# Four cross attentions of a perceiver: new orders of the steps in the masked and plain ones, one query operand for all, values one group at a time

## The reference

```python
q = split_heads(query @ wq_kernel + wq_bias)         # query: layernorm of x
k = split_heads(key @ wk_kernel + wk_bias)           # key, value: context, 4096 tokens
v = split_heads(value @ wv_kernel + wv_bias)
scores = jnp.einsum('bhqd,bhkd->bhqk', q, k) / jnp.sqrt(jnp.float32(HD))
scores = jnp.where(m == 0, jnp.float32(-1000000000.0), scores)   # layer 1: m = mask
attn = jax.nn.softmax(scores, axis=-1)
out = jnp.einsum('bhqk,bhkd->bhqd', attn, v)
return out @ wo_kernel + wo_bias
```

## Time and profile before

| | us |
|---|---|
| median of three runs | 1549.96 |
| lowest, highest run | 1547.44, 1559.05 |
| the profiled execution, as timed | 1559.34 |
| its span in the trace | 1558.1 |
| PE busy | 1348.7 (87%) |
| DVE busy | 1008.2 (65%) |
| ACT busy | 849.9 (55%) |
| POOL busy | 518.1 (33%) |

### The profile page before, as it was taken

The page is one execution under the profiler, slowest core; times in us unless marked ns, Lnnn a source line. Parts: engine busy times, 40 slices in busy tenths (PEclk is TensorE's granted clock), DMA queues, the critical chain, the costliest instruction groups (busy, mean ns, idle before and its releaser), DMA issues. The chain is left out here.

```text
span 1558.1 us, 28950 instructions
## 1 busy us (share of the span) xinstructions
PE 1348.7 (87%) x10520; PEld 684.5 (44%) x10594; DVE 1008.2 (65%) x2341; ACT 849.9 (55%) x1302; POOL 518.1 (33%) x700
## 2 busy tenths in 40 slices
PE   6879999799999888599999888599998895999987
PEld 3536567233333356234444455234444582344445
DVE  3524656899999634678886043588885236888832
ACT  1121211799999621189999451167777211777762
POOL 1322011498998810655665330111110002111100
PEclk8989999699999887699999899779999996899999
DMA  6376787111114020111113146112225201112400
GB/s 212 117 223 213 218 252 240 55 43 42 46 36 130 1 68 1 45 52 47 50 49 121 62 120 212 49 37 58 61 62 187 68 0 37 52 52 56 119 2 7
DMA packets 115679, 136.35 MB, mean 88 GB/s; under 512 B 13729, under 2 KB 96841, under 8 KB 113490
## 3 DMA queue, kind: packets, MB, share of 16 engines
q1 hardware_dynamic: 100434, 117.95, 24.4%
q10 hardware_dynamic: 15104, 16.56, 3.7%
HBM read 99.55 MB, written 34.87 MB: 86 GB/s over the span
## 5 line engine op out<-in xcount | busy, mean ns | idle before, releaser
L1150 ACT ACTIVATE prob_a<-ps 128x1024 f32<-128x1024 f32 x464 | 457.5, 1021 | 131.3 <-PE ps L978 90.6
L960 PE MATMUL ps<-kop,qop 52*128 52x512 f16 x1024 | 312.1, 418 | 57.2 <-DVE best_a L1174 19.1
L1174 DVE TENSOR_REDUCE best_a<-ps 128x1 f32<-128x512 f32 (+1 forms) x488 | 315.2, 709 | 52.5 <-PE ps L960 52.2
L978 PE MATMUL ps<-qop,kop 52*128 52x256 f16 x2048 | 246.6, 281 | 6.3 <-ACT prob_a L1150 3.7
L1007 PE MATMUL ps<-prob_a,vop_a 128*32 128x256 f32 x3072 | 211.9, 414 | 7.7 <-ACT qop L1090 3.1
L960 PEld LDWEIGHTS ps<-kop,qop 52*128 52x128 f16 x1024 | 77.0, 95 | 266.8 <-DVE best_a L1174 92.7
L1170 DVE CUSTOM_DVE_ANT_0 dump_a<-ps,neg_q 128x512 bf16<-128x512 f32 (+1 forms) x244 | 163.6, 715 | 43.3 <-PE ps L960 42.0
L1288 POOL TENSOR_TENSOR used_a<-prob_a,gT 128x1024 f32<-128x1024 f32 x64 | 153.0, 2391 | 27.9 <-DVE used_a L1187 17.0
L1266 POOL TENSOR_SCALAR mrest_a<-nmax_a 128x2 f32<-128x2 f32 x64 | 27.8, 434 | 354.2 <-DVE nmax_a L1179 352.9
L978 PEld LDWEIGHTS ps<-qop,kop 52*128 52x128 f16 x2048 | 96.4, 96 | 95.2 <-issue 30.8
L554 ACT ACTIVATE kp<-ps,bk 128x512 f16<-128x512 f32 x64 | 43.8, 687 | 171.1 <-PE ps L486 156.7
(11 more groups left out here) (367 smaller groups left out, 1783.7 us busy)
## 6 DMA issues: line engine op xcount, KB each, us to landing
kop<-kparts SPq DMA_DIRECT2D x384, 64.0 KB, 2.3
vals<-vst SPq DMA_DIRECT2D x16, 1024.0 KB, 4.4
kparts<-kp SPq DMA_DIRECT2D x64, 256.0 KB, 2.3
vraw<-vals SPq DMA_DIRECT2D x64, 256.0 KB, 3.0
e_w<-in_e_w SPq DMA_DIRECT2D x4, 2048.0 KB, 11.8
z_w<-in_z_w SPq DMA_DIRECT2D x24, 256.0 KB, 6.8
ctxT<-in_ctxT SPq DMA_DIRECT2D x8, 512.0 KB, 12.3
raw<-in_mask ACTq DMA_DIRECT2D x16, 256.0 KB, 4.1
```

The costliest lines, as they stand in the source:

```text
L960: return pe.matmul(out, qop[rows, h, t * P:(t + 1) * P], kop[rows, h % UNROLL, first:first + CHUNK], start=True, stop=True)
L978: ins = pe.matmul(st_bank(n)[:, j * NT:(j + 1) * NT], kop[rows, h % UNROLL, at:at + P], qop[rows, h, :], start=(j % 2 == 0), stop=(not add ...
L1150: act.activation(prob[:, n % NP, :], st_bank(n), ACT.Exp, scale=1.0 / SCORE_UNIT).then_inc(S("exp_done"), 1)
L1174: dve.tensor_reduce(out, bank, AX.X, ALU.max).then_inc(sem, 1)
```

## The change

1. The order strings of the masked and the plain attention are new, and with them `SUM_AT` and `TURN_AT` (after which exponential ACT reads the sums and places the maxima). In the plain one values come one group at a time in four places ("v") and two by two ("vv") in two.
2. The masked attention shields two groups a head, not three: g = 1 and 5. The third gets two mask matmuls instead (L983).
3. `qop` is one tile for all layers, set to zero once, by POOL, in `project_context`. For layers 1 to 3 only the rows that hold more than loads write are cleared, by two small DMAs of zeros from DRAM (`clear_rows`), and PE waits for them before its first product, and in layer 2 for the row of ones of the mask too, for which SP waited at its end before.
4. Queries that see no key get zeros in the query operand. In layer 0 POOL multiplies the whole of `qop` (4096 values a partition) by a 0/1 tile at the end of `project_context`. In layer 1 DVE first writes the masked sum to `whole` (two instructions), ACT copies it into the high part and DVE subtracts for the low part.
5. The mask's number is -2^27, not -2^100, in the cross attentions.

```diff
-MASKED_ORDER = "CCK CCK CCK CVV CCK KCCKF CKCT KCCC VV".replace(" ", "")
-PLAIN_ORDER = "CCKCKCCV CCKCKCV CKCCT KF CKCCKC VV".replace(" ", "")
+MASKED_ORDER = "CCKKCCV CCKKCCCV CKKCF CTKCCV KCCV".replace(" ", "")
+PLAIN_ORDER = "CCKCKv CCvKCCKv CCvKCCKKFTCCK CvvCCvv".replace(" ", "")
...
+    def clear_blind(self, dve, S, banks, whole, sighted):
+        for mt in range(CT):
+            dve.wait_ge(S("q_psum"), mt + 1)
+            dve.scalar_tensor_tensor(out=self.half(whole, mt), in0=self.c.ps[:, banks[mt], 0:NT],
+                                     scalar=self.c.bq[:, self.l, mt:mt + 1], in1=sighted[:, :],
+                                     op0=ALU.add, op1=ALU.mult).then_inc(S("q_whole"), 1)
+    def high_of(self, act, S, whole):
+        for mt in range(CT):
+            act.wait_ge(S("q_whole"), mt + 1)
+            act.activation(self.half(self.qp[:, HIGH, :], mt), self.half(whole, mt), ACT.Copy).then_inc(S("q_part0"), 1)
+    def low_of(self, dve, S, whole):
+        for mt in range(CT):
+            dve.wait_ge(S("q_part0"), mt + 1)
+            dve.tensor_tensor(self.half(self.qp[:, LOW, :], mt), self.half(whole, mt), self.half(self.qp[:, HIGH, :], mt),
+                              ALU.subtract).then_inc(S("q_part1"), 1)
...
                     if u == 2 * EARLY:
+                        sp.wait_ge(S("qop_set"), 1)
+                        sp.dma_start(c.clear_rows, c.qop[R_MAX:R_LOW, :, :]).then_inc(S("clear_kept"), 16)
                         q.load_half(sp, S, 0)
...
-            dve.memset(c.qop[:, 0:UNROLL, :], 0.0).then_inc(S("qop_set"), 1)
...
-            pool.memset(c.qop[:, UNROLL:H, :], 0.0).then_inc(S("qop_rest_set"), 1)
+            pool.memset(c.qop[:, :, :], 0.0).then_inc(S("qop_set"), 1)
...
+                    if l == 3 and i == PIECES - 1:
+                        pool.wait_ge(S("blind_loaded"), 16)
+                        pool.tensor_scalar(sighted[:, :], blind, -1.0, 1.0, ALU.mult, ALU.add).then_inc(S("sighted"), 1)
+                        pool.wait_ge(S("sighted"), 1)
+                        pool.wait_ge(c.ops.S("q_first"), Q_DONE)
+                        pool.wait_ge(c.ops.S("q_rest"), Q_DONE)
+                        pool.tensor_tensor(c.qop[:, :, :], c.qop[:, :, :], sighted[:, :].unsqueeze(1).to_broadcast((P, H, NT)), ALU.mult)\
+                            .then_inc(S("sighted"), 1)
...
     def _(dve):
         norm_dve(c, dve, S, c.x, c.xn)
-        dve.memset(c.qop[:, 0:UNROLL, :], 0.0).then_inc(S("qop_set"), 1)
...
     def _(pool):
         norm_pool(c, pool, S)
-        pool.memset(c.qop[:, UNROLL:H, :], 0.0).then_inc(S("qop_rest_set"), 1)
...
     def _(sp):
+        for half in range(HALVES):
+            at, rows = half * HROWS + R_MAX, (R_MASK if l == KEYED else R_LOW) - R_MAX
+            sp.dma_start(c.qop[at:at + rows, :, :], c.clear_rows[0:rows, :, :]).then_inc(S("rows_cleared"), 16)
...
-    SUM_AT, TURN_AT = (1, 1) if weighted else (2, 5) if by_query else (3, 5)
-    SHIELD = (2, 5, 7) if l == SHIELDED else ()
+    SUM_AT, TURN_AT = (1, 1) if weighted else (3, 4) if by_query else (4, 5)
+    SHIELD = (1, 5) if l == SHIELDED else ()
...
-        if l == KEYED:
-            sp.wait_ge(asked.S("mask_placed"), 16 * HALVES)
...
+        if asked is not None:
+            pe.wait_ge(asked.S("rows_cleared"), 16 * HALVES)
+        if l == KEYED:
+            pe.wait_ge(asked.S("mask_placed"), 16 * HALVES)
...
-                elif step == "V":
+                elif step in "Vv":
+                    many = 2 if step == "V" else 1
                     if n >= 0:
-                        two_values(n)
-                    n += 2
+                        some_values(range(n, n + many))
+                    n += many
```

More of the change, by code:

```diff
@@ L36 @@
 SOFTMAX_FILL, SCAN_FILL = 12, 12
-NEG = -(2.0 ** 100)
+NEG = -(2.0 ** 27)
+FRAME_NEG = -(2.0 ** 100)
 E = 8
@@ L415, in project_context @@
         blind = c.xn[:, 0, :]
+        sighted = sb("sighted", [P, NT], F32)
         best_seen = c.xn[:, 1, 0:QT * 4].rearrange("p (t i) -> p t i", t=QT)
@@ L475, in _ @@
             sp.wait_ge(S("g_loaded"), 16 * NGROUP)
+            sp.wait_ge(S("clear_kept"), 16)
         @block.tensor
@@ L808, in queries @@
     blind = sb("blind", [P, NT], BF16) if l == SHIELDED else None
+    sighted = sb("sighted", [P, NT], F32) if l == SHIELDED else None
+    whole = sb("whole", [P, CT * NT], F32) if l == SHIELDED else None
     stage = Stage(S)
@@ L814, in _ @@
         norm_dve(c, dve, S, c.x, c.xn)
-        dve.memset(c.qop[:, 0:UNROLL, :], 0.0).then_inc(S("qop_set"), 1)
-        q.low(dve, S, banks)
         if l == SHIELDED:
             dve.wait_ge(S("masks_summed"), 1)
+            dve.tensor_scalar(sighted[:, :], c.ps[:, 7, 0:NT], (KEYS - 0.5) * NEG, None, ALU.is_gt).then_inc(S("sighted"), 1)
             dve.tensor_scalar(blind[:, :], c.ps[:, 7, 0:NT], (KEYS - 0.5) * NEG, None, ALU.is_le).then_inc(S("blind_found"), 1)
+            dve.wait_ge(S("sighted"), 1)
+            q.clear_blind(dve, S, banks, whole, sighted)
+            q.low_of(dve, S, whole)
+        else:
+            q.low(dve, S, banks)
     @stage.gpsimd
@@ L846, in _ @@
            .then_inc(S("xT_ready"), 1)
-        q.high(act, S, banks)
+        if l == SHIELDED:
+            q.high_of(act, S, whole)
+        else:
+            q.high(act, S, banks)
         q.load_half(act, S, 1)
@@ L1010, in values, with some_values @@
             ins.then_inc(S("pv_psum"), 1)
-        def two_values(first):
-            for n in (first, first + 1):
+        def some_values(groups):
+            for n in groups:
                 if n % NGROUP == 0:
@@ L1803, in _ @@
             pool.wait_ge(S("mask"), 1)
-            pool.memset(mask[0:FR, FR:2 * FR], NEG).then_inc(S("mask"), 1)
-            pool.memset(mask[0:FR, P + 3 * FR:P + 4 * FR], NEG).then_inc(S("mask"), 1)
+            pool.memset(mask[0:FR, FR:2 * FR], FRAME_NEG).then_inc(S("mask"), 1)
+            pool.memset(mask[0:FR, P + 3 * FR:P + 4 * FR], FRAME_NEG).then_inc(S("mask"), 1)
             add_bias_pool(c, pool, S, bo)
@@ L2753, in program @@
         c.vals = nc.dram_tensor("vals", (LAYERS, P, KT * D), F32).ap()
+        c.clear_rows = nc.dram_tensor("clear_rows", (R_LOW - R_MAX, H, NT), F16).ap()
         c.ops = Operands(c, ctx)
+        c.qop = sb("qop", [P, H, NT], F16)
         steps = 12 if steps is None else steps
@@ L2803, in cross @@
         if l > 0:
-            c.qop = ctx.enter_context(c.nc.sbuf_tensor(f"qop{l}", [P, H, NT], F16))
             asked = queries(c, l, ctx)
```

25 lines of the change are left out of this document (10 added, 15 removed).

## The result

The changed kernel takes **1508.6 us** (median of 4 runs, 1506.1 to 1510.9), the kernel before on the same chip 1553.2 (median of 4, 1547.4 to 1559.1). The ratio is 0.971, with a 95% interval of 0.967 to 0.976. That is 44.6 us less where 23.3 were forecast. The profiled execution of the changed kernel took 1510.9 around a span of 1509.6; that of before was as long as the longest of its four, with a span of 1558.1. So the two traces differ by 48.5.

The account below looks back on a forecast made before the run. DVE was nearest its limit in plain heads (10.35 us of 11.55, the rest stalls), PE busiest in masked ones. Terms -11.7 - 2.0 - 4.7 - 8.0 + 0.5 + 2.6 = -23.3 took 1549.96 to 1526.7 us, range 1506 to 1547.

Parts of the forecast that it names:

- Stretches and waits of the plain head: Plain attention: laying out one head gave 11.1 us for 11.55, 0.45 less in each of 26 heads, -11.7.
- The seven heads with the low clock I leave at their number and price: Plain attention: seven of 26 heads at granted clock 0.50, 1.7 us longer each, were assumed to stay so.
- Rival B: Plain heads reach DVE's floor or the clock stays up: -12 or -19, total 1508 to 1515; chance 0.13.
- Masked heads: Masked attention: PE becomes the bound at 13.1 to 13.2 us a head against 13.31, -2.0 over 13 heads.
- The end: End of masked attention: last group no longer shielded, -3.2, and last head and a half by ACT, -1.5; together -4.7.
- Starts of layers 1 to 3: Without POOL's large memset, everything up to the first C comes 2.66 us sooner per layer: -8.0, bounds -6 and -10.
- One more DVE instruction of 0.48: Start of layer 1: the query passes DVE, ACT, DVE instead of ACT, DVE, costing +0.5 us.
- The product over `qop`: End of keys and values: POOL's product ends 2.5 us after DVE did, +2.6; bounds 0 and +4.2.
- The execution that the difference was taken from: The profiled execution, 1559.34 us, was the slowest of three; the forecast subtracted from their median, 1549.96.
- Rival A: Plain attention: F is the new wait, heads return to 11.55 and gain nothing; total -11.6, 1538; chance 0.20.
- Rival C: Plain attention: the clock falls in all 26 heads, not 7: +32, 1559, slower than before; chance 0.09.
- Rival D: Masked attention: no mask overlaps, heads take 13.8 us, +8.5 against -2, total 1535; chance 0.08.

Follow-up runs that it names:

- the early fold: Changed kernel with F and T one key product earlier in the plain order and the sums read after g = 3: 1498.0 us, ratio 0.966.
- the block of four: Changed kernel with single value groups joined into pairs, then the last two pairs joined into one block of four groups: 1570.9 us (one run).
- A's order: A is the changed kernel itself, with its new order strings: 1508.6 us, run again 1510.6 us.

## Why the prediction was right, and where it was not

The side, faster by over 1%, and the range hold. The range held narrowly, by 2.6 us at its lower end, and the change was nearly twice the forecast one. The number was 18 too high. The fall was 21 more than forecast, and the median that it was taken from rose by 3 with a fourth run. The steps:

- **Stretches and waits of the plain head**: right. Predicted 11.1 with 0.28 at the division and 0.48 after it; measured 11.05 with 0.40 at the division and 0.30 of small delays. The layout from a block's price of 0.66 holds (0.64), and the chain named is the one that waits: the early fold takes it away. 26 x 0.5 = -13 for -11.7.
- **"The seven heads with the low clock I leave at their number and price"**: the step that failed. They are 2 now, at 1.6 each, for 7 at 1.65: -8.4. That is five fewer, just the number up to which the forecast was to stand. Rival B gave this -12 and had 0.13. Its counter-argument, that the stretch with T and F is still there, was true and did not decide: the stretch is there and shorter, 3.5 for 4.0. The changed order has 10 low-clock heads in 182 (seven traces), the old one 13 in 52 (two traces), the early fold none in 78 (three traces), and the block of four 22 in 26. What in the order does it stays open.
- **First and last plain heads**: not costed at all. In the traces the first division comes 1.5 and 1.7 sooner (39.0 and 39.4 after the stage's start; the kernel with the old order back has 40.2 and 41.1, so this goes with the order), the last two distances are 2.4 and 0.2 shorter, and the 13th is 10.84 for 11.55 (-0.4 net in the layout of 11.05). Together -6. With -13 and -8.4 this makes the -27.6 of the table. Most of the -2.4 is a drop more or less: the last distance of A's order is 5.4 at full clock and 7.1 with the low clock in it, and both occur from run to run.
- **Masked heads**: 13.18 for a predicted 13.1 to 13.2, with PE the bound. The end was -5.1 over the last three distances, predicted -4.7.
- **Starts of layers 1 to 3**: the term of 2.66 was mis-sized, 4.5 and 4.2 in layers 2 and 3, and 11.0 for the three in the run with the memset back, outside the bound of 10. (`xn` itself took 1.8 to 2.0, where 1.8 or less was to be the sign.) The trace held the missing piece: some 2.9 of idle PE ahead of the transpose and 0.50 of clock in the projection behind it. I had followed the wait to the first C as a mere shift in time.
- **"One more DVE instruction of 0.48" in layer 1**: mis-sized too. The chain got 2.5 of waiting for POOL's product besides. The -2.2 of that start agrees with the forecast only because this and the missing clock term cancel.
- **The product over `qop`**: +1.5 for +2.6. The mechanism was right (POOL ends last). The time of one value was 1.95 ns for 2.07, and the next stage starts 0.3 after POOL's last instruction, where I had carried over the 1.0 that it takes after DVE's.
- **The execution that the difference was taken from**: the traces differ by 48.5, the medians by 44.6. Taking the sum from the median of before was right, since its trace had a drop in an unchanged stage (one head of the weighted attention of 18.2 for 16.0).
- **Rival A** (F takes all back) fell: F's chain costs 0.40 and no more. **Rival C** (more drops of the clock) fell for this order, by -5 heads for +19, but the block of four shows that an order can do it: 1570.9. **Rival D** (13.8 in the masked heads) fell here. The same 13.84 came with another order, by a wait for ACT and not by masks that don't overlap.

The sum with the measured terms: plain heads -13, drops of the clock -8.4, first and last heads -6.2, masked attention -7, starts -10.9, product +1.5, makes -44.0, against 44.6 between the medians. The middle terms carry two or three microseconds of scatter each, so the agreement is better than it has a right to be. Taking one part back at a time gives a second account between medians: plain order 29.0, masked order 11.4, memset 12.5, product -3.2, together 49.7. It is 5 over the whole, and that much such sums can be off.

One rule that the prediction weighed: the Trainium skill, TensorE: Matmul & The Clock Gate, section A second HAM failure mode: psum-queue depth-cycling, says that small pauses between groups of matmuls while the banks are cycled make the clock oscillate. By it, more and smaller blocks would have meant more drops. The runs show the contrary: with blocks of 8 and 16 matmuls 10 low-clock heads in 182, with blocks up to 32 matmuls 13 in 52. What went with drops was a longer stretch without values, in two orders with a dense block behind it.

## What to carry to other kernels

Where a granted clock of 0.50 shows in some heads of a trace, look at what PE does in the microseconds before it falls, not only at the block that it makes longer, and try an order that leaves a shorter stretch without dense work there: the fewer drops were worth 8 us here beside the 13 of the shorter heads, though no run shows whether the stretch or the block counts. A wait of PE ahead of a projection can cost its length and then the projection at half clock: price both. When a chain is taken off the path, lay out the next one before you count the gain. The early fold won 0.28 a head, not 0.65, since a wait behind the placed maxima came next.
